# GpSimd waits inside a graph network kernel: sorted edges scattered three at a time, and early gathers held to TensorE's turns

## The reference

```python
edge_index = jnp.stack([src, dst])
x = _layernorm(x + _L0_gnn_ref(x, ..., edge_index), axis=-1)   # 3 GRU steps: agg = segment_sum(m[src], dst)
x = _layernorm(x + _L1_gnn_ref(x, edge_index, ...), axis=-1)   # hypergraph: two segment sums, batch norm
x = _layernorm(x + _L2_gnn_ref(x, edge_index, ...), axis=-1)   # attention: softmax over src of leaky_relu(s1[src] + s2[dst])
x = _layernorm(x + _L3_gnn_ref(x, edge_index, ...), axis=-1)   # edge MLP per edge, summed by dst, node MLP
```

## Time and profile before

| what | us |
|---|---|
| median of 3 timed runs | 4749.77 |
| lowest and highest of them | 4746.3, 4755.25 |
| span of the profiled execution | 7303.0 |
| pass 4, undisturbed, in the profile | 327 |
| GRU stages behind pass 0 and behind pass 1, in the profile | 918 and 87 |

### The profile page before, as it was taken

How to read it: one execution, slowest core, us unless ns; L and a number is a source line. 1 busy time by engine, 2 the same in 40 slices (tenths; PEclk the granted TensorE clock), 3 DMA queues, 4 the chain that set the end, 5 groups by cost and what they waited for, 6 DMA issues and landing times. The chain is left out here.

```text
span 7303.0 us, 82736 instructions
## 1 busy us (share of the span) xinstructions
PE 4076.2 (56%) x24237; PEld 3354.5 (46%) x24238; DVE 3381.7 (46%) x7886; ACT 2340.3 (32%) x3120; POOL 2658.9 (36%) x2706
## 2 busy tenths in 40 slices
PE   4332641019981111117989798988672197666655
PEld 2111420007761101106778586858571197665644
DVE  4222540358970000106788776456451076555545
ACT  0000010005640000004555455557461075444433
POOL 4555157730017777770000000000427601444463
PEclk7665865559995555558999898989785598888777
DMA  9400000009970000116658287843444343444432
GB/s 376 155 0 0 0 2 0 0 23 334 368 250 0 0 0 0 28 25 222 232 189 293 96 293 214 296 162 95 132 125 124 97 139 98 132 132 130 130 95 67
DMA packets 364823, 923.20 MB, mean 126 GB/s; under 512 B 114026, under 2 KB 138716, under 8 KB 364531
## 3 DMA queue, kind: packets, MB, share of 16 engines
q1 hardware_dynamic: 214722, 650.09, 26.9%
q10 hardware_dynamic: 58609, 180.13, 6.4%
q0 software_dynamic: 91200, 89.42, 5.2%
HBM read 705.69 MB, written 213.71 MB: 126 GB/s over the span
## 5 line engine op out<-in xcount | busy, mean ns | idle before, releaser
L1741 POOL DMA_INDIRECT edges_halves<-local,gather_idx x832 | 854.9, 1027 | 791.7 <-SPq L372 505.4
L1680 POOL DMA_INDIRECT adj_t<-cell_val,cell_at x832 | 828.6, 996 | 465.2 <-issue 369.9
L862 PE MATMUL ps<-tiles_r,stage_r 128*128 128x512 f32 x2028 | 811.6, 400 | 158.2 <-issue 132.0
L1134 POOL DMA_INDIRECT big<-table,gather_idx x576 | 548.4, 952 | 832.3 <-DVE stage L1284 376.3
L869 PE MATMUL ps<-stage,big 128*128 128x130 f32 x4046 | 520.1, 284 | 370.3 <-issue 354.7
L1134 POOL DMA_INDIRECT x_fm<-table,gather_idx x384 | 370.2, 964 | 959.8 <-DMA table<-cell_at 689.7
L869 PEld LDWEIGHTS ps<-stage,big 128*128 128x128 f32 x4046 | 497.9, 199 | 388.5 <-issue 384.6
L2059 PE MATMUL ps<-big,ident_h 128*128 128x104 bf16 (+1 forms) x2880 | 359.7, 256 | 460.4 <-issue 459.7
L1253 PE MATMUL ps<-big,stage 128*128 x1920 | 356.2, 342 | 352.7 <-issue 189.3
L1319 PE MATMUL ps<-ident,big 128*128 128x128 f32 x260 | 73.3, 377 | 817.2 <-issue 768.2
L2442 DVE TENSOR_TENSOR big<-ps,stage 128x1248 bf16<-128x1248 f32 x192 | 270.7, 1451 | 519.5 <-remote 385.1
(11 more groups left out here) (482 smaller groups left out, 9007.8 us busy)
## 6 DMA issues: line engine op xcount, KB each, us to landing
onehot<-adj_t SPq DMA_DIRECT2D x332, 512.0 KB
big<-adj_t SPq DMA_DIRECT2D x332, 512.0 KB
onehot<-adj_s SPq DMA_DIRECT2D x170, 512.0 KB
adj_t<-rows ACTq DMA_DIRECT2D x13, 6656.0 KB
adj_s<-big ACTq DMA_DIRECT2D x157, 512.0 KB, 5.3
stage<-local_rows SPq DMA_DIRECT2D x120, 512.0 KB
big<-adj_s SPq DMA_DIRECT2D x84, 512.0 KB
x_fm<-adj_s SPq DMA_DIRECT2D x84, 512.0 KB
```

The source lines that it names most:

```text
L862: nc.tensor.matmul(psum_fm(p, n)[:, 0:cut], upper_rows[:, k, :], tile[:, 0:cut], start=k == 0, stop=False, skip_group_check=True)
L1134: return nc.gpsimd.indirect_dma_start(out, None, table[0:N, :], bass.IndirectOffsetOnAxis(gather_idx[:, t:t + 1], 0))
L1680: nc.gpsimd.indirect_dma_start(out, bass.IndirectOffsetOnAxis(cells[:, c:c + 1], 0), cell_val[:, c:c + 1], None).then_inc(S(name), 16)
L1741: nc.gpsimd.indirect_dma_start(edges_halves, bass.IndirectOffsetOnAxis(slot_at[:, at:at + 1], 0), slot_val[:, at:at + 1], None).then_inc(h ...
```

## The change

Two constants and two waits, both on POOL's queue.

```diff
+EARLY_FROM, EARLY_TURNS = 50, 5 / 2
+SORTED_TOGETHER = 3
...
                 for u in range(2 * CH):
+                    if u % CH == 0:
+                        used = EARLY_FROM + math.floor(EARLY_TURNS * (2 * k + u // CH))
+                        pool.wait_ge(S("tile_used"), turns_before(len(MODES) - 1) + min(used, PASS_TURNS))
                     if u == CH // 2 and k > 0:
                         store(k - 1)
...
                     nc.gpsimd.indirect_dma_start(edges_halves, bass.IndirectOffsetOnAxis(slot_at[:, at:at + 1], 0),
                                                  slot_val[:, at:at + 1], None).then_inc(halves_written[n % 2].sem, 16)
+                    if (c + 1) % SORTED_TOGETHER == 0:
+                        wait(pool, halves_written[n % 2], 16 * (SLW * (n // 2) + c + 1))
```

## The result

The changed kernel takes 5188.95 us (median of 4 runs, 5185.66 to 5191.07) beside 4750.75 us for the kernel before beside it (median of 4, 4746.3 to 4755.25): ratio 1.0926, 95% interval 1.0911 to 1.0942, so **438 us slower**. The forecast was 161 us slower, 4911, with a range up to 5080. Direction and place were right, the size was not.

What follows compares the result with a forecast made beforehand. Timed runs: passes bound by PE at full clock, edge stage by DVE, POOL's queue critical only where slack ends. Sorted scatter +149 and early gathers +12 make 161 on 4749.8, so 4911 us; range 4715 to 5080.

Steps and rivals of the forecast that it cites:

- The profile of before: Whole kernel: span 7303.0 us, 2553 over the timed runs, because PE hardly moves beside POOL's indirect DMAs under profiling only.
- The undisturbed lengths: Held stages at their unheld length: GRU stage 87 us, pass 1 325, attention pass 668, edge stage 782, first stretch 1400.
- The window: From the first sorted scatter to DVE's need of the pairs in pass 4: 1316 us available in a timed execution.
- A three, unloaded: Sorted scatters on POOL: three with their wait cost 5.31 us instead of 3.81, all 1465 us.
- A three beside the loads: Sorted scatters in three passes with tile loads: also 5.31 us; upper bound 1.27 more for some 175 waits, +371.
- The argument from 4 B elements: Sorted scatter's landing: small elements, 4 B against the row's 512, speak for somewhat less than 2.77 us, load for more.
- What the stall costs: Pairs' gathers at pass 4: scatters exceed the available time by 149 us, DVE and PE wait, +149 us all on the path.
- Part two: Early gathers in pass 5: first waits for turn 50, 13 us later; 2.5 turns don't bind; +12 us, 13 at most.
- A (nothing waits): Sorted scatters and early gathers: POOL's issues or landings are shorter, three cost 4.2 us; 4750 to 4762 us, chance 0.20.
- B (faster): PE beside POOL's stream: part of the hold exists in timed runs, waits free 20 to 60 us; 4690 to 4730, chance 0.17.
- C (landing long under load): Sorted scatters beside loads in three passes: landings take longer, +371 and 12 us; 5000 to 5130 us, chance 0.18.
- the held span: Changed kernel's profile: PE is held too, but less, so its span may fall while timed runs get longer.

Runs made afterwards that it cites:

- the second profile: The kernel before, unchanged, profiled a second time: measured once at 4745.41 us, span 4743.7.
- sorted alone: The changed kernel with only the waits of the sorted scatter, behind every third, early gathers as before: 5183.99 us, ratio 1.0919 to the kernel before.
- 13 at a time: Sorted alone with SORTED_TOGETHER 13, so a wait behind every 13th sorted scatter: 4745.99 us, ratio 1.0003 to the kernel before.
- sixes: Sorted alone with SORTED_TOGETHER 6, so a wait behind every sixth sorted scatter: 4921.47 us, ratio 1.0362 to the kernel before.

## Why the prediction was wrong

**The profile of before.** The reading that its 2553 us too many are PE held beside POOL, and that timed runs have none of it, is right. Profiling alone doesn't bring the hold, since the second profile has none. The undisturbed lengths put in its place were partly wrong, in opposite directions. The first stretch, up to the GRU stage, takes 1217 us, not the 1400 that were left over. The edge stage takes 902, not 782: its last chunks go at POOL's pace, some 10 us each, and even the others at 6.9, while the rows behind the 6.52 were of one place. The stage behind pass 5 takes 105, not 47, pass 5 itself 648 (3042.2 to 3690.6), not 668, and passes 1 and 2 338 each, not 325. A sum that is closed with a remainder proves little.

**The window.** 1316 us were forecast. In the undisturbed profile the first scatter is at 1226.89 and DVE needs the pairs at 2580.35; less 12 for the gathers and their landing this is 1342. In the changed kernel it is 1779 less the stall, 1329. This term held, to 13 and 26 us.

**A three, unloaded.** Forecast 5.31, measured 4.98 to 5.2. Held, slightly too high. By the 2.0 us of the Trainium skill (DMA: Bandwidth & Descriptors, Anatomy of one DMA) the estimate was 4.54 us and no stall at all; the trace has 4.98, between it and the row's 5.31.

**A three beside the loads: the step that failed.** The forecast took the same 5.31 for all 272 waits, and put one issue spacing more, 1.27, as upper bound under load. Measured it is 2.6 to 2.9 us more than unloaded, twice that bound. The sum again with what was measured: about 122 of the waits fall in passes 1 to 3 at some 7.9 us, 964; 150 outside them at 5.1, 765; 22 for the scatters without a wait and 21 for the one long landing: 1772, for the 1779 measured and the 1465 forecast. Against 1329 that is a stall of 443 to 450. The argument from 4 B elements, which was set against the load and left the term at its unloaded size, was the wrong way to choose: with these 4 B elements a landing beside the loads still took twice as long. What the scatter's own bytes do was not varied.

**What the stall costs.** All on the path, as forecast: PE does nothing for 400 us in the windows. 12 us come back in passes 1 and 2, which take 332 and 331 where the stream of before makes it 338. Pass 2 of sorted alone:

```profile
1731.90:2062.70 330.80, 319.56 (x1355) 255.91 (x1355) 265.84 (x655) 177.92 (x170) 136.62 (x127) 0.97 0.84 279
```

**Part two.** Forecast +12, bound 13; measured +5 (interval 1 to 10). In the undisturbed profile the first gather starts 192 us into the pass, when PE has done 1542 products; with the wait for turn 50 it is 200 us and 1622 products. So the start was 7 to 8 us later, not 13. The pace of 2.5 turns didn't bind. The deadline was the last store, as forecast, but the one who waits is ACT in the stage behind pass 5, ahead of its copies into `x_fm`; SP's wait came later. In the kernel before that wait is 77 us already: pass 5 ends 20 us earlier than forecast, and the last store is issued 544 us behind the first gather, not 523. So there was no point of balance, and nearly every microsecond of start counts. That the forecast of +12 came near the +5 is in part luck: it let the last store and the start of the edge stage just meet, and they are 77 us apart.

**The rivals.** A (nothing waits) is false: even beside idle DMA engines a three takes 4.98 us, not 4.2, and where no stall came, with 13 at a time, POOL still stood for 231 us inside its slack. B (faster) is false in size: fewer scatters give back 6 us each in passes 1 and 2 and none in pass 3. C (landing long under load) was the right mechanism, but its 5000 to 5130 too lies under the 5189 measured, since its bound was taken from an unloaded spacing. Of the signs named for the profile, the held span did not appear; beside the undisturbed 4743.7 the span rose with the timed runs.

## What to carry to other kernels

Price a wait for a DMA's landing at the DMA share of the stretch in which it lies; a landing seen beside idle DMA engines is a lower bound. Here, at a share of 0.85, POOL stood 4.1 us on average for the landing behind a three, where it stood 1.5 us beside idle DMA engines. When POOL's stream has a deadline, write down its slack first (here 238 us with the stage behind it), divide it by the cost of a wait (here 3.5 us, 226 us for 64), and that is how many waits are free: some 68, where the change has 272. When a profile's span is not that of the timed runs, take another profile before building on reconstructed stages.

## What the runs showed of the hardware

One profiled execution can hold PE wherever POOL streams indirect DMAs (918 us for a stage of 97.5), and all the others of the same and of nearly the same code not at all. What sets it off, no run here tells.

One landing took 22.6 us in sorted alone, in the stage behind pass 3. The DMA queues between 2515 and 2550 us, the view of the DMA between 2540 and 2541 us, the timelines of SP and POOL, and SP's wait for its own store read:

```profile
q1 hardware_dynamic: 6672, 0.03, 62.2%
...
degree_row<-small SPq DMA_DIRECT2D x1, 26.0 KB
...
DMA packets 0, 0.00 MB, mean 0 GB/s; under 512 B 0, under 2 KB 0, under 8 KB 0
...
2517.34 0.40 SPq L1571 DMA_DIRECT2D degree_row<-small  x1
...
2543.10 0.97 POOL L1743 DMA_INDIRECT edges_halves<-local,gather_idx  x1 [22.63 <-DMA edges_halves<-local,gather_idx]
...
SPq L374 <- DMA degree_row<-small: 24.9, 1, 24.9
```

SP issues a store of 26 KB in 4-byte elements, over 6600 packets. Its packets are through by some 2536 us, and from 2538 to 2543 the trace has no packet at all; yet the store's landing and that of the three scatters issued beside it, from another engine, both come only at some 2543. In the second profile of before only the 8 gathers of the pairs are beside it, and no scatter, and SP waits 27.4 us for the same store: so the store is as slow without scatters, and the scatters wait it out. What holds the landing in its last 5 to 7 us isn't shown. Every kernel here with waits in threes or sixes has this one long wait (21.1 to 25.3 us), and with 13 it is the 13.8 us that POOL stands ahead of the pairs' gathers.
